# The last part of a decoder layer: weighting, adding and normalizing in five pieces of 2, 4, 4, 4 and 2 token tiles

## The reference

```python
x = layernorm(x + self_attention(x))            # 16 heads of 16, causal
x = layernorm(x + cross_attention(x, ctx_768))  # 16 heads of 64, 64 context rows
x = layernorm(x + ffn(x))

# ffn: mixture of experts, 8 experts, top 2
logits = xt @ Wg.T
topk_logits, topk_idx = top_k(logits, 2)
w = softmax(topk_logits)                        # the two gates of each token
h = gelu(einsum('th,ehi->tei', xt, W1) + b1)
o = einsum('tei,eih->teh', h, W2) + b2
y = einsum('te,teh->th', gates, o)              # sum over the token's two experts

# layernorm(x) = (x - mean) / sqrt(var + 1e-5), over the 256 values
```

## Time and profile before

| what | value |
|---|---|
| runs | 821.57, 831.28, 823.75 us; median 823.75 |
| the profiled execution's own time | 822.79 us |
| its span, first to last instruction | 821.0 us |
| instructions | 13771 |
| busy: PE, DVE, ACT, POOL | 634.1, 551.6, 394.3, 332.2 us |
| loads of `parts` issued | from 787.5 us |
| last store issued | at 816.5 us |

### The profile page before, as it was taken

The page is one execution under the profiler, slowest core; times in us unless marked ns, Lnnn a source line. Parts: engine busy times, 40 slices in busy tenths (PEclk is TensorE's granted clock), DMA queues, the critical chain, the costliest instruction groups (busy, mean ns, idle before and its releaser), DMA issues. The chain is left out here.

```text
span 821.0 us, 13771 instructions
## 1 busy us (share of the span) xinstructions
PE 634.1 (77%) x4988; PEld 421.2 (51%) x4988; DVE 551.6 (67%) x956; ACT 394.3 (48%) x599; POOL 332.2 (40%) x367
## 2 busy tenths in 40 slices
PE   5687748769877798776688758537999999999970
PEld 3554422235622346222353335425998898898950
DVE  6556514556765458545383338696999999999764
ACT  3543544424355234442145513105687777777524
POOL 9212332324533245232243423315556545664225
PEclk9989777779998689986699969756999999999975
DMA  9909552009810197100711000354778877886263
GB/s 289 180 22 166 194 192 92 1 13 174 124 51 0 19 177 112 52 1 0 105 52 52 2 0 1 105 202 151 253 253 300 292 256 257 289 289 226 78 214 113
DMA packets 79562, 109.82 MB, mean 134 GB/s; under 512 B 5240, under 2 KB 67392, under 8 KB 78472
## 3 DMA queue, kind: packets, MB, share of 16 engines
q1 hardware_dynamic: 75760, 98.83, 43.2%
q0 software_dynamic: 3744, 10.23, 3.4%
HBM read 87.08 MB, written 21.95 MB: 133 GB/s over the span
## 5 line engine op out<-in xcount | busy, mean ns | idle before, releaser
L1008 ACT ACTIVATE probs<-R 128x1024 f32<-128x1024 f32 (+3 forms) x128 | 86.5, 704 | 102.0 <-PE R L1249 101.8
L360 DVE TENSOR_REDUCE rowmax<-G 128x1 f32<-128x384 f32 (+3 forms) x132 | 78.6, 637 | 70.1 <-PE G L350 70.1
L333 PE MATMUL HB<-xT,w 128*128 128x256 f16 (+1 forms) x1104 | 110.0, 261 | 5.7 <-DVE xT L1850 5.7
L1614 POOL DMA_INDIRECT scratch_ys<-y,dst x39 | 75.7, 1941 | 83.9 <-DVE y L1865 78.2
L1991 PE MATMUL YB<-w,h 128*128 128x256 f16 x936 | 105.9, 273 | 0.9 <-issue 0.9
L333 PEld LDWEIGHTS HB<-xT,w 128*128 128x128 f16 x1104 | 95.7, 99 | 18.2 <-DVE xT L1850 7.7
L949 POOL TENSOR_SCALAR_AFFINE_SELECT probs<-probs 128x256 f32<-128x256 f32 x128 | 51.8, 411 | 123.1 <-ACT probs L1008 122.7
L1695 ACT ACTIVATE hf<-HB,b 128x256 f32<-128x256 f32 (+1 forms) x184 | 71.4, 439 | 57.7 <-PE HB L333 53.6
L1991 PEld LDWEIGHTS YB<-w,h 128*128 128x128 f16 x936 | 91.4, 98 | 11.5 <-issue 1.2
L1259 PE MATMUL PV<-probs,v_aug 128*32 128x128 f32 (+3 forms) x512 | 59.9, 545 | 5.4 <-POOL probs L949 5.4
L345 PE MATMUL G<-ks_m,qs_m 64*128 64x128 f16 (+3 forms) x192 | 28.8, 345 | 39.7 <-DVE rowmax L360 32.4
(11 more groups left out here) (265 smaller groups left out, 1076.9 us busy)
## 6 DMA issues: line engine op xcount, KB each, us to landing
w1f<-in_W SPq DMA_DIRECT2D x23, 1024.0 KB
w2f<-in_W SPq DMA_DIRECT2D x23, 1024.0 KB
scratch_qk<-qk SPq DMA_DIRECT2D x8, 512.0 KB, 4.6
scratch_ax<-stage SPq DMA_DIRECT2D x16, 256.0 KB, 2.8
scratch_vw<-stage SPq DMA_DIRECT2D x16, 256.0 KB, 3.4
a_x<-scratch_ax SPq DMA_DIRECT2D x4, 1024.0 KB, 6.6
vw<-scratch_vw SPq DMA_DIRECT2D x4, 1024.0 KB, 4.8
parts<-scratch_ys SPq DMA_DIRECT2D x8, 512.0 KB, 7.4
```

The source lines that it names most:

```text
L333: last = nc.tensor.matmul(out, left(a, k), right(b, k), start=(k == 0 and m == 0), stop=(k == n - 1 and m == 2))
L360: return nc.vector.tensor_reduce(k["rowmax"][:, t, par * PAIRS + p0:par * PAIRS + p0 + pairs], bank[:, 0:pairs * wide].rearrange("p (n w) ...
L1008: A.activation(probs[:, n % 4, :, 0:S - 128 * j], R[slot][:, :, 0:S - 128 * j], ACT.Exp, scale=1.0 / (QS * QS)).then_inc(r.empty[slot], 1)
L1614: pool.indirect_dma_start(out=dram["ys"], in_=y[:, n % 2, t, :], in_offset=None, out_offset=bass.IndirectOffsetOnAxis(dst[:, at:at + 1], 0 ...
```

## The change

The last part goes in five pieces, `SPANS`, of 2, 4, 4, 4 and 2 token tiles. There are ten loads (four of 256 KB, six of 512 KB) and five stores (two of 256 KB, three of 512 KB). For pieces 0 to 3 the order of adding is turned round: DVE adds the first expert's part when it has landed and the bias is in (`weighed(k, 0)`, `first_added`), and POOL adds the second expert's part, weighted by ACT, behind it (`add_part`); DVE waits for POOL only before the moments. Piece 4 is added by DVE alone, both parts. `root` has two independent `tensor_scalar` instructions, then the power, then one product, where there were four instructions in a row. The small buffers hold all 16 tiles, so the wait on `z_done` in DVE's list is gone. The order on each engine becomes:

- DVE: bias 0, bias 1; first part of 0, first part of 1; bias 2, moments 0, first part of 2; bias 3, moments 1, first part of 3; both parts of 4; moments 2, 3, 4.
- POOL: add 0; add 1, root 0; add 2, root 1; add 3, root 2; root 3; root 4.
- ACT: weigh 0, 1; weigh 2, normalize 0; weigh 3, normalize 1; normalize 2, 3, 4.

```diff
-    power = sb("power2", [128, 3 * NQ])
-    shift = sb("shift", [128, 2, NQ])
+    power = sb("power2", [128, NQ])
+    shift = sb("shift", [128, NT])
...
+    SPANS = [(0, 2), (2, 6), (6, 10), (10, 14), (14, 16)]
+    LAST = len(SPANS) - 1
...
-        for k in range(NT // NQ):
+        for k, (a, b) in enumerate(SPANS):
             for c in range(2):
-                sp.dma_start(parts[:, k * NQ:(k + 1) * NQ, c, :], dram["ys"][c * T + k * S:c * T + (k + 1) * S, :]
+                sp.dma_start(parts[:, a:b, c, :], dram["ys"][c * T + a * 128:c * T + b * 128, :]
                              .rearrange("(t p) d -> p t d", p=128)).then_inc(parts_in[k], 16)
...
-        P.memset(power[:, 0:NQ], EPS).then_inc(const_step, 1)
-        P.memset(power[:, NQ:2 * NQ], -0.5).then_inc(const_step, 1)
-        P.memset(power[:, 2 * NQ:], -1.0).then_inc(const_step, 1)
+        P.memset(power[:, :], -0.5).then_inc(const_step, 1)
...
         def add_part(k):
 
-            rows = slice(k * NQ, (k + 1) * NQ)
-            pool.wait_ge(bias_added, 2 * k + 2)
-            pool.wait_ge(part_done, k)
+            rows = slice(*SPANS[k])
+            pool.wait_ge(first_added, k + 1)
+            pool.wait_ge(part_done, k + 1)
             P.tensor_tensor(z[:, rows, :], z[:, rows, :], parts[:, rows, 1, :], ALU.add).then_inc(part_added, 1)
 
         def root(k):
 
+            rows, size = slice(*SPANS[k]), SPANS[k][1] - SPANS[k][0]
             pool.wait_ge(var_done, k + 1)
-            P.tensor_tensor(rstd[:, k % 2, :], meanvar[:, k % 2, :, 1], power[:, 0:NQ], ALU.add).then_inc(pool_step, 1)
-            pool.wait_ge(pool_step, 3 * k + 1)
-            P.tensor_tensor(rstd[:, k % 2, :], rstd[:, k % 2, :], power[:, NQ:2 * NQ], ALU.pow).then_inc(pool_step, 1)
+            P.tensor_scalar(rstd[:, rows], meanvar[:, rows, 1], EPS, None, ALU.add).then_inc(pool_step, 1)
+            P.tensor_scalar(shift[:, rows], meanvar[:, rows, 0], -1.0, None, ALU.mult).then_inc(pool_step, 1)
             pool.wait_ge(pool_step, 3 * k + 2)
-            P.tensor_tensor(shift[:, k % 2, :], rstd[:, k % 2, :], meanvar[:, k % 2, :, 0], ALU.mult).then_inc(pool_step, 1)
+            P.tensor_tensor(rstd[:, rows], rstd[:, rows], power[:, 0:size], ALU.pow).then_inc(pool_step, 1)
             pool.wait_ge(pool_step, 3 * k + 3)
-            P.tensor_tensor(shift[:, k % 2, :], shift[:, k % 2, :], power[:, 2 * NQ:], ALU.mult).then_inc(rstd_done, 1)
-
-        for k in range(1, NT // NQ):
+            P.tensor_tensor(shift[:, rows], shift[:, rows], rstd[:, rows], ALU.mult).then_inc(rstd_done, 1)
+
+        add_part(0)
+        for k in range(1, LAST):
             add_part(k)
             root(k - 1)
-        root(NT // NQ - 1)
+        root(LAST - 1)
+        root(LAST)
...
-        for k in range(1, NT // NQ):
+        weigh(0)
+        weigh(1)
+        for k in range(2, LAST):
             weigh(k)
-        for k in range(NT // NQ):
+            normalize(k - 2)
+        for k in range(LAST - 2, LAST + 1):
             normalize(k)
...
+        def weighed(k, c):
+
+            dve.wait_ge(parts_in[k], 2 * 16)
+            for t in range(*SPANS[k]):
+                last = V.scalar_tensor_tensor(z[:, t, :], parts[:, t, c, :], gate[:, c, t:t + 1], z[:, t, :],
+                                              ALU.mult, ALU.add)
+            return last
+
+        def moments(k):
+
+            for t in range(*SPANS[k]):
+                last = V.bn_stats(stats[:, t, :], z[:, t, :])
+            after(last)
+            for t in range(*SPANS[k]):
+                last = V.bn_aggr(meanvar[:, t, :], stats[:, t, :])
+            last.then_inc(var_done, 1)
+
+        add_bias(0)
+        add_bias(1)
+        dve.wait_ge(bias_added, 4)
+        weighed(0, 0).then_inc(first_added, 1)
+        weighed(1, 0).then_inc(first_added, 1)
+        for k in range(2, LAST):
             add_bias(k)
...
+            dve.wait_ge(part_added, k - 1)
+            moments(k - 2)
+            dve.wait_ge(bias_added, 2 * k + 2)
+            weighed(k, 0).then_inc(first_added, 1)
+        for c in range(2):
+            after(weighed(LAST, c))
+        for k in range(LAST - 2, LAST):
+            dve.wait_ge(part_added, k + 1)
+            moments(k)
+        moments(LAST)
```

More of the change, by code:

```diff
@@ L1449, in expert_block @@
     y = sb("y", [128, 2, 2, D])
-    power = sb("power2", [128, 3 * NQ])
-    shift = sb("shift", [128, 2, NQ])
+    power = sb("power2", [128, NQ])
+    shift = sb("shift", [128, NT])
     parts = sb("parts", [128, NT, 2, D])
-    stats = sb("stats2", [128, NQ, 6])
-    meanvar = sb("meanvar2", [128, 2, NQ, 2])
-    rstd = sb("rstd2", [128, 2, NQ])
+    stats = sb("stats2", [128, NT, 6])
+    meanvar = sb("meanvar2", [128, NT, 2])
+    rstd = sb("rstd2", [128, NT])
+    SPANS = [(0, 2), (2, 6), (6, 10), (10, 14), (14, 16)]
+    LAST = len(SPANS) - 1
     HB = [ctx.enter_context(nc.psum_tensor(f"HB{i}", [128, 2, SLOTS], F32)) for i in range(4)]
@@ L1488, in expert_block @@
     hot_done = sem("hot_done")
-    parts_in = [sem(f"parts_in{i}") for i in range(NT // NQ)]
+    parts_in = [sem(f"parts_in{i}") for i in range(len(SPANS))]
+    first_added = sem("first_added")
     part_done, part_added = sem("part_done"), sem("part_added")
@@ L1550, in _ @@
         sp.wait_ge(y_out[1], blocks_upto(TILES - 2))
-        for k in range(NT // NQ):
+        for k, (a, b) in enumerate(SPANS):
             for c in range(2):
-                sp.dma_start(parts[:, k * NQ:(k + 1) * NQ, c, :], dram["ys"][c * T + k * S:c * T + (k + 1) * S, :]
+                sp.dma_start(parts[:, a:b, c, :], dram["ys"][c * T + a * 128:c * T + b * 128, :]
                              .rearrange("(t p) d -> p t d", p=128)).then_inc(parts_in[k], 16)
-        for k in range(NT // NQ):
+        for k, (a, b) in enumerate(SPANS):
             sp.wait_ge(z_done, k + 1)
-            sp.dma_start(dram["out"][k * S:(k + 1) * S, :].rearrange("(t p) d -> p t d", p=128),
-                         z[:, k * NQ:(k + 1) * NQ, :]).then_inc(stored, 16)
-        sp.wait_ge(stored, NT // NQ * 16)
+            sp.dma_start(dram["out"][a * 128:b * 128, :].rearrange("(t p) d -> p t d", p=128),
+                         z[:, a:b, :]).then_inc(stored, 16)
+        sp.wait_ge(stored, len(SPANS) * 16)
     @block.gpsimd
@@ L1578, in _ @@
         P.iota(own_i[:, :], pattern=[[128, BLOCKS]], base=0, channel_multiplier=1).then_inc(const_step, 1)
-        pool.wait_ge(const_step, 13)
+        pool.wait_ge(const_step, 11)
         P.affine_select(out=before[:, :], in_=before[:, :], compare_op=ALU.is_ge, fill=1.0, base=0,
@@ L1713, in weigh @@
             act.wait_ge(parts_in[k], 2 * 16)
-            for t in range(k * NQ, (k + 1) * NQ):
+            for t in range(*SPANS[k]):
                 last = A.activation(parts[:, t, 1, :], parts[:, t, 1, :], ACT.Copy, scale=gate[:, 1, t:t + 1])
@@ L1719, in normalize @@
             act.wait_ge(rstd_done, k + 1)
-            for t in range(k * NQ, (k + 1) * NQ):
-                last = A.activation(z[:, t, :], z[:, t, :], ACT.Identity, bias=shift[:, k % 2, t % NQ:t % NQ + 1],
-                                    scale=rstd[:, k % 2, t % NQ:t % NQ + 1])
+            for t in range(*SPANS[k]):
+                last = A.activation(z[:, t, :], z[:, t, :], ACT.Identity, bias=shift[:, t:t + 1], scale=rstd[:, t:t + 1])
             last.then_inc(z_done, 1)
@@ L1901, in add_bias @@
                 V.tensor_tensor(z[:, rows, :], bank[:, :, :], z[:, rows, :], ALU.add).then_inc(bias_added, 1)
-        for k in range(NT // NQ - 1):
-            add_bias(k)
[L1905 to L1929, removed]
```

## The result

The changed kernel takes 825.57 us (median of 22 runs, 820.86 to 834.14), the kernel before 821.96 us (22 runs, 818.64 to 831.28). Run against run the ratio is 1.0042, with a 95% interval of 1.0023 to 1.0060: 3.5 us slower (1.9 to 4.9). Forecast were +1.4 us, 824.2 us, and no change by 2%. The sign and the main cause came out as forecast; the size was short by 2 us.

A forecast was written before the change was run, and what follows sets the result against it. DVE and POOL were taken to bound, nearly together, the 33.5 us after the last scatter. Saved DVE instructions and an earlier start gave -0.9 us, the collision +2.35: 822.79 + 1.4 = 824.2 us, range 820.8 to 827.0.

The forecast's parts named there:

- The collision: POOL's add 3 beside DVE's multiply-adds of pieces 3 and 4: holds the last two, costing 2.35 us; chance 0.50.
- eight multiply-adds without a break: DVE's four multiply-adds of piece 3 and four of piece 4, taken as unbroken, until 806.9 us if not held.
- no collision: Rival: POOL's add 3 and DVE's multiply-adds do not hold each other on SBUF; 821.9 us, chance 0.20.
- POOL stands: Rival: POOL's add 3 waits until DVE's eight multiply-adds are done, at 806.95; 822.5 us, chance 0.13.
- the term of 794.5 us: Loads after the last scatter: piece 1 lands at 794.5 us, like the third load before, with 1.5 MB moved.
- By bytes: Basis for load landings: bytes moved set the pace, not the number of loads; piece 1 in at 794.5 us.
- The rival: Landings go by count of loads: piece 1 in at 795.9 us, everything behind 1.4 later; 825.6 us, chance 0.12.
- The lock to the letter: Rival: the powers in POOL's roots 0 and 1 also hold DVE's multiply-adds, +1.8 us; 826.0 us, chance 0.05.
- The shorter root: POOL's rearranged root could save one step of 0.2 us or nothing; costed as nothing.
- The end: Finish of the kernel: last store lands at 820.8 us against 819.4, +1.4 us, giving 824.2 us.
- Root 3 and root 4 fit under it: POOL's last two roots, ending about 814.9 and 816.5 us, run under ACT's ten normalizations, which last until 818.2.

The follow-up runs named there:

- e5: Changed kernel with pieces of 4, 2, 4, 4 and 2 tiles, large loads first; ratio 1.0050 to the kernel before, 37.1 us from last scatter to end.
- e7: Kernel before with one more fill on POOL behind its last root, which nothing waits for; 35.3 us from last scatter to end, where it was 33.5.
- e4: Kernel before, its last block ending without the drain of POOL's queue; ratio 1.0004 to the kernel before, 32.4 us from last scatter to end.
- e1: Changed kernel with POOL's add of piece 3 replaced by a fill that reads nothing from SBUF; 34.2 us from last scatter to end, where it was 36.2.
- e10: Changed kernel run once more without an edit, for another trace of its loads; 36.6 us from last scatter to end.
- e3: Changed kernel, its last block ending without the drain of POOL's queue; ratio 1.0031 to the kernel before, 35.6 us from last scatter to end.

## Why the forecast was right, and where it was short

- **The collision: right.** Place, partner and kind are as forecast: add 3 starts after root 1, 2.4 us after moments 1, gets in between two multiply-adds and holds DVE. It came at 807.1, behind six of the eight multiply-adds: the seventh ended at 809.7 and the eighth stood behind it, the two that the forecast had named. The "eight multiply-adds without a break" have one, at just this place, which the forecast did not see. The cost was 2.12 us where the term was 2.35. The rivals "no collision" and "POOL stands" fall with the 2606 ns, while add 3 kept its 2.34 us.
- **The loads: the term of 794.5 us failed.** By bytes piece 1 should have been in at 7.0 us; it was 7.93 in the profiled execution, up to 9.3 in others. The rival had the effect (slower by up to 1.4) but not the reason: e5 shows that a fourth load can land at 7.0.
- **The lock to the letter: rightly set aside.** The power of root 1 (1.12 us) ran beside multiply-adds of 476 and 477 ns.
- **The shorter root: rightly costed at nothing.** It still has four instructions. The last root of four tiles beside no multiply-add takes 1.94 us (814.11 to 816.05), where it was 1.86.
- **The end: the step that failed.** I wrote "Root 3 and root 4 fit under it", meaning ACT's normalizations, and added 1.6 us to the landing of the last store. The store landed at 33.7 us after the scatter, against 33.3 forecast and 31.9 before: +1.8, near the forecast +1.4. But POOL's last instruction moved from 26.9 to 29.6 us, +2.7, and that is what the span follows (e7, e4). Five pieces put one more root at POOL's end, and the smaller last store brought nothing, since it is not what is waited for. The forecast's own schedule has root 4 end at 816.5, 29.0 us after the scatter and 2.1 later than the last root before; with the end put there the sum would have been +2.1 and not +1.4, and the rival without collision (root 2 done 2.3 us earlier, at 810.7) about -0.2 and not -0.9. The rows of the drain were in the trace of the kernel before.

The ledger from trace to trace is 2.7 us, at POOL's last instruction. Of these, 2.1 are in the forecast's own schedule. The other 0.6 are where its terms were off: at the end of the multiply-adds DVE is 0.15 us behind it (piece 1 came 0.95 late, but the hold and the steps before it were shorter), and each of the three roots behind them took about 0.1 longer than costed, with its gaps.

Singly, the collision gives back 2.0 (e1). A late load passes through whole: with the fourth load in at 7.9, 8.3 and 9.3 us (changed, e10, e3) POOL's last instruction ends at 29.6, 29.9 and 31.0. So the lateness of 0.95 in the profiled execution is worth about 0.95; this is worked out, and no run takes out the late load or the fifth root and leaves the rest as it is. Without both the stretch would be about 33.2 us, 0.3 under that of before. The runs show 3.5 us and not 2.7; the 2.7 lie inside their interval, and later landings in other executions (up to 1.4 more) pull the same way.

## What to carry to other kernels

Before two engines are made to work side by side, look for a place in the trace where these two kinds of instruction already overlap and read their durations there; here a 414 ns instruction that took 2464 told what a reordering would cost. Follow the end of the program past the last store to the rows of the sequencers: work on POOL that nobody waits for can still end the span. A small first transfer meant to start the work sooner can make the next one late.

## What was not expected of the hardware

- POOL's queue needs 6.7 us to drain at the end of the expert block, in which it had issued 78 indirect DMAs. The drain ends 6.5 us after POOL's last instruction. At the end of the two earlier blocks, without such DMAs, it took 2.2 and 0.8 us but ended less than 0.1 us after POOL's last instruction. That the DMAs are the cause is inferred, not tested.
- Two loads of 256 KB ahead of loads of 512 KB delay the landing of the first 1.5 MB from 7.0 to between 7.9 and 9.3 us.
